# Scores as three fp32r products, exponentials kept in PSUM, and the last weights stored by chunk, in the cross attention of a fused perceiver block

## The chip, the cores and the metric

The kernel runs on one core of a Trainium2 chip. The metric is device time in microseconds (us), lowest is best, as the median of several runs. TensorE (PE in the profile) multiplies, VectorE (DVE), ScalarE (ACT) and GpSimd (POOL) work element by element, and SyncE (SP) issues nearly all DMAs.

## The reference

The whole function is a block on x of 64 batches x 32 rows x 512: a cross attention against a context of 257 rows x 128 per batch, then a self attention with small rank, then a feed-forward part. The change touches the cross attention alone. Cut to what matters, for one batch and 16 heads:

```python
q_big = rope(einsum("shk,hkq->shq", hidden_q @ Wq.T, w_kc_q))
kv_r  = rope(kv_c)                                  # 257 x 128
scores = einsum("hsr,hlr->hsl", q_big @ W_qr, kv_r @ W_kr)
attn  = softmax(scores, axis=-1)                    # over 257 positions
ctx_c = einsum("hsl,ld->hsd", attn, kv_r)           # 32 x 128 for each head
out   = concat_heads(ctx_c @ w_kc_kv.T) @ Wo.T      # 32 x 512, added to x
```

## The kernel before, in words

`query_path` (0 to 459 us) folds the query weights and both key weights, so that for every batch b there are finished queries of 128 x 512: 128 features on the partitions, 16 heads x 32 rows along the free side. They are written to an internal DRAM tensor (`carried_queries`), but the last two heads stay in SBUF, in `staged`, a part of `x1`. In its last units ACT copies the last two heads of batches 0 and 1 straight into `crossing.q` (L565). `fp32r` is a 4-byte format that TensorE multiplies in one pass; an fp32 product is kept accurate with it by splitting each operand into a rounded high part and a rest (low), and adding three products, high x high, high x low and low x high: `multiply_parts` (L65).

`cross_attention` (460 to 964 us) goes through 64 batches in 16 tiles of four (u = 0 to 3). A batch has two halves (steps); n = 2b + half counts the 128 steps. A step handles 8 heads as two blocks c of 128 rows. TensorE's program for step n is, in this order:

- `score(n+1)` (L1061): two fp32 matmuls, 128 queries x 257 keys, into two PSUM banks of `sc_ps`. Four banks exist, so steps alternate between two pairs. It waits for the exponentials of step n-1.
- `turn_weights(n)` (L1071): four transposes of the normalised weights `e` (positions 0 to 255) into `et_ps`. It waits for `normed` of n and for `et_split` of n-1.
- in half 1 `turn_kv` of the next batch; then a share of the output projection of an earlier tile (3 heads in half 1, 1 head in half 0, nine or three fp32r matmuls of 512 columns), and in half 0 `mix` of the batch before (six fp32r matmuls).

VectorE's program for step n: `find_peak(n+1)` (L892), `keep_ends(n)` (L906, the weight of position 256 out of `e`), in half 0 `split_kv`, in half 1 `add_end` of the batch before (L922, which adds position 256's share and needs its weights spread over all partitions), `normalise(n+1)` (L897), `split_turned(n)` (L913), and once in a tile `add_out` (L932). ScalarE's: `exponential(n+1)` (L997), `round_turned(n)` (L1006), in half 1 `round_kv` and `round_mixed` (L1018). GpSimd turns the keys of batch b + 2 in half 0 (`rotate`, L861, three operations) and makes the low part of the mixed values in half 1 (`split_mixed`, L872). SyncE (L829) issues in order for each batch: the store of the end weights of four batches back (2 KB, L821), three loads of raw keys (L707), the spread of those end weights out of DRAM to 128 partitions (L827), two loads of queries (L840, L841); once in a tile a load of x. After the last tile it issues five loads of weights for the self attention into `spare` (`holo.load`, L674), and only then the stores and spreads of the last four batches. All engines run their queues strictly in order, and nothing is planned by cost: the order is written out by hand.

Raw keys have four buffers, queries four, turned keys four, `ends` and `ends_spread` two.

Of the kernel before, what the change touches and what calls it, by code (L numbers as in the profile page):

```python
# [18 lines left out]
ALU = mybir.AluOpType  # L19
ACT = mybir.ActivationFunctionType  # L20
# [59 lines left out]
def query_path(nc, x_s, early, w_qr, w_kr, late, angle_q, centre_q, x1, spare, crossing, ident, eps, w_vo_dram, q_dram):  # L80
# [7 lines left out]
    with ExitStack() as ctx:  # L88
# [80 lines left out]
        def _(sp):  # L169
# [91 lines left out]
            crossing.output_weights(sp, w_vo_dram, 2)  # L261

# [252 lines left out]
        def _(act):  # L515
# [43 lines left out]
            def store_qc(U, J, sign):  # L559
                base = BASES[J][sign]  # L560
                for ab in range(2):
                    act.wait_ge(carried, 4 * U + 2 * sign + ab + 1)
                    if isinstance(U, int) and U >= 2 * HPAIRS - 2:
                        at = (H - 2 + ab) * S + base
                        nc.scalar.activation(crossing.q[:, :, at:at + G], ps[:, QC_BANK + ab].rearrange("p (b s) -> p b s", b=B)[:, 0:2], ACT.Copy)  # L565
# [117 lines left out]
class Crossing:  # L683


    def __init__(self, nc, ctx, cache_t, rope_kv):
# [4 lines left out]
        raw, swapped = sb("c_raw", [P, 2, L]), sb("c_swapped", [P, 2, L])  # L691
        self.raw, self.swapped = ([a[:, u] for u in range(2)] for a in (raw, swapped))

        self.q = sb("c_q_first", [P, 2, H * S])
        self.keys = sb("c_keys_first", [P, L])
        self.q_loaded = [sem(f"c_q_loaded{u}") for u in range(BT)]
        self.pool_chained, self.rotated = sem("c_pool_chained"), sem("c_rotated")
        self.table_loaded = sem("c_table_loaded")
        self.raw_loaded = [sem(f"c_raw_loaded{u}") for u in range(BT)]
# [14 lines left out]
    def first_queries(self, sp, q_dram):  # L714

        for u in range(2):
            sp.dma_start(self.q[:, u, 0:(H - 2) * S], q_dram[u, :, 0:H - 2].rearrange("d h s -> d (h s)")).then_inc(self.q_loaded[u], 16)
# [8 lines left out]
    def rotate_first(self, nc, pool, part):  # L726
# [3 lines left out]
        nc.gpsimd.tensor_tensor(part[:, 1], self.swapped[0], self.table[:, 1], ALU.mult).then_inc(self.pool_chained, 1)  # L730
        pool.wait_ge(self.pool_chained, 2)
        nc.gpsimd.tensor_tensor(self.keys[:], part[:, 0], part[:, 1], ALU.add).then_inc(self.rotated, 1)
# [7 lines left out]
def cross_attention(nc, crossing, holo, x, q_dram, w_vo_dram, ends_dram, x1, stat, ident, eps, half_pi, left_counted):  # L740
# [4 lines left out]
    with ExitStack() as ctx:  # L745
# [7 lines left out]
        raw_later, swapped_later = sb("c_raw_later", [P, BT - 2, L]), sb("c_swapped_later", [P, BT - 2, L])  # L753
        crossing.raw += [raw_later[:, u] for u in range(BT - 2)]
        crossing.swapped += [swapped_later[:, u] for u in range(BT - 2)]
        table, raw, swapped = crossing.table, crossing.raw, crossing.swapped
        table_loaded, raw_loaded = crossing.table_loaded, crossing.raw_loaded
        part = sb("c_part", [P, 2, L])
        kv_later = sb("c_kv_t", [P, BT - 1, L])
# [38 lines left out]
        def queries_in(u, t):  # L798

            return 32 * t + (16 if u < 2 else 32)  # L800
# [1361 lines left out]
```

## Time and profile before

| | us |
|---|---|
| median of 3 runs | 1603.71 (1599.01 to 1604.7) |
| the profiled execution: own time / span | 1602.14 / 1600.3 |
| mean granted TensorE clock of it | 0.972 |
| PE / DVE / ACT / POOL busy | 1482.6 / 1151.1 / 810.9 / 514.5 |
| cross attention, first scores to last projection | 460 to 964 |

The profile is of one execution. A share of busy time is an average over very different stages, and matmuls are pipelined, so their recorded durations overlap: the pace is read from the distance between two starts. A row of the timeline has the start, the time covered, the engine, the line of the code, what is written and read, and how many instructions were merged into it. An fp32 matmul shows as two records.

### The profile page before, as it was taken

Reading aid. Unit: us, or ns where it says so; the run is one execution under the profiler, and the core shown is the slowest. Engines: PE = TensorE matmul, PEld = TensorE weight load, DVE = VectorE, ACT = ScalarE, POOL = GpSimd, SP = SyncE. Lnnn points to the kernel's source line nnn. Section 1 sums busy time; section 2 is a strip of 40 time slices with the busy share of each in tenths; the row PEclk is TensorE's granted clock in tenths of the full one; section 3 lists DMA queues with packets and bytes.
Section 4 is the critical chain, followed back from the end, with each engine's and each line's share of the span. In section 5 each row is a group of like instructions: output and inputs, shape, how many; then the busy total and the mean of one; then the engine's idle time right before and its main releaser. Section 6 shows DMA issues by size and latency. Waiting matters only on the chain. (4 is left out here: it accounts for less than half of the span.)

```text
span 1600.3 us, 26575 instructions
## 1 busy us (share of the span) xinstructions
PE 1482.6 (93%) x8136; PEld 1122.0 (70%) x8136; DVE 1151.1 (72%) x2076; ACT 810.9 (51%) x1739; POOL 514.5 (32%) x466
## 2 busy tenths in 40 slices
PE   5799999999967999999999977999898899999997
PEld 3577777777746778777787756888443478787876
DVE  6888777887649888888888753767687735656466
ACT  4566566656545555555555433555211355554554
POOL 4244333542024444444444313221351202222021
PEclk9899999999999999999999988999898899999999
DMA  4223334243575555555555514000244100000000
GB/s 153 70 83 107 105 110 125 73 123 90 187 210 117 114 120 111 131 108 125 112 121 115 127 20 172 0 0 0 84 175 159 43 1 1 27 1 26 0 27 27
DMA packets 140918, 140.06 MB, mean 88 GB/s; under 512 B 84150, under 2 KB 111926, under 8 KB 139708
## 3 DMA queue, kind: packets, MB, share of 16 engines
q1 hardware_dynamic: 140284, 138.54, 32.5%
q10 hardware_dynamic: 576, 0.81, 0.2%
q8 instruction: 29, 0.48, 0.1%
q14 instruction: 29, 0.24, 0.0%
HBM read 109.88 MB, written 27.39 MB: 86 GB/s over the span
## 5 line engine op out<-in xcount | busy, mean ns | idle before, releaser
L1002 ACT ACTIVATE c_e<-c_sc_ps,c_peak 128x257 f32<-128x257 f32 x256 | 119.6, 472 | 215.3 <-DVE c_peak L895 215.3
L874 POOL TENSOR_TENSOR c_mixed_low<-c_whole,c_mixed_high 128x512 fp32r<-128x512 f32 x64 | 81.6, 1275 | 256.8 <-ACT c_mixed_high L1022 256.8
L77 DVE TENSOR_TENSOR b_rot_parts_low<-b_rot,b_rot_parts_high 128x1536 fp32r<-128x1536 f32 x64 | 136.5, 2132 | 21.9 <-ACT b_rot_parts_high L541 21.9
L1578 PE MATMUL f_ps<-f_right,f_left 128*128 128x512 f32 x256 | 115.5, 613 | 8.7 <-ACT f_raw L1621 6.3
L278 POOL TENSOR_TENSOR b_turned_raw<-b_turn_part 128x384 f32<-128x384 f32 x32 | 70.0, 2189 | 164.4 <-DVE b_key_parts_low L77 163.2
L895 DVE TENSOR_REDUCE c_peak<-c_sc_ps 128x2 f32<-128x514 f32 x128 | 88.5, 691 | 44.9 <-PE c_sc_ps L1068 43.4
L70 PE MATMUL c_out_ps<-c_shared_high,c_mixed_high 128*128 128x512 f32 x256 | 112.4, 439 | 8.5 <-issue 8.5
L324 DVE TENSOR_TENSOR b_rot<-b_w_qr,b_angle 128x1536 f32<-128x1536 f32 x64 | 118.6, 1852 | 0.2
L70 PE MATMUL b_ps<-c_shared_high,b_wq_parts_high 128*128 128x512 f32 x256 | 108.4, 423 | 6.5 <-DVE c_shared_low L77 6.5
L70 PE MATMUL e_mm_ps<-folded_high,e_h_t_high 128*128 128x512 f32 x256 | 106.4, 416 | 5.7 <-DVE e_h_t_low L77 5.6
L541 ACT ACTIVATE b_rot_parts_high<-b_rot 128x1536 fp32r<-128x1536 f32 x64 | 95.2, 1488 | 24.5 <-PE b_ps L72 17.0
L274 POOL TENSOR_TENSOR b_turn_part<-b_early,b_centre 128x384 f32<-128x384 f32 x64 | 83.8, 1329 | 71.5 <-DMA b_early<-early 69.9
L1934 ACT ACTIVATE spare<-spare 128x512 f32<-128x512 f32 x64 | 46.3, 724 | 114.0 <-DVE spare L2001 114.0
L72 PE MATMUL b_ps<-c_shared_high,b_wq_parts_low 128*128 128x512 f32 x256 | 103.5, 404 | 0.0
L1076 PE MATMUL c_et_ps<-ident,c_e 128*128 128x128 f32 x512 | 79.6, 278 | 25.8 <-DVE c_e_t_low L77 24.8
L71 PE MATMUL b_ps<-c_shared_low,b_wq_parts_high 128*128 128x512 f32 x256 | 103.0, 402 | 0.0
L72 PE MATMUL e_mm_ps<-folded_high,e_h_t_low 128*128 128x512 f32 x256 | 102.6, 401 | 0.0
L71 PE MATMUL e_mm_ps<-folded_low,e_h_t_high 128*128 128x512 f32 x256 | 102.4, 400 | 0.0
L71 PE MATMUL c_out_ps<-c_shared_low,c_mixed_high 128*128 128x512 f32 x256 | 102.3, 400 | 0.0
L72 PE MATMUL c_out_ps<-c_shared_high,c_mixed_low 128*128 128x512 f32 x256 | 102.3, 400 | 0.0
L1578 PEld LDWEIGHTS f_ps<-f_right,f_left 128*128 128x128 f32 x256 | 50.1, 197 | 73.9 <-issue 65.2
L1076 PEld LDWEIGHTS c_et_ps<-ident,c_e 128*128 128x128 f32 x512 | 57.1, 141 | 60.5 <-DVE c_e L903 31.3
(232 smaller groups left out, 3937.2 us busy)
## 6 DMA issues: line engine op xcount, KB each, us to landing
c_ends_spread<-end_weights SPq DMA_DIRECT2D x64, 256.0 KB, 3.8
carried_queries<-x SPq DMA_DIRECT2D x7, 2048.0 KB, 11.3
b_early<-early SPq DMA_DIRECT2D x15, 640.0 KB, 4.0
f_left<-ent_in SPq DMA_DIRECT2D x16, 512.0 KB, 5.2
f_right<-ent_out SPq DMA_DIRECT2D x16, 512.0 KB, 6.5
c_q_first<-carried_queries SPq DMA_DIRECT2D x32, 224.0 KB, 3.3
c_q<-carried_queries SPq DMA_DIRECT2D x32, 224.0 KB, 3.4
b_late<-late SPq DMA_DIRECT2D x16, 320.0 KB, 3.8
```

What stands on the lines that cost most here:

```text
L70: nc.tensor.matmul(out, left[0], right[0], start=start, stop=False)
L71: nc.tensor.matmul(out, left[0], right[1], start=False, stop=False)
L72: return nc.tensor.matmul(out, left[1], right[0], start=False, stop=stop)
L77: return nc.vector.tensor_tensor(low, value, high.bitcast(F32), ALU.subtract)
L274: nc.gpsimd.tensor_tensor(turn_part[:, n], key, centre[:, 2 * v + n].unsqueeze(2).to_broadcast(shape), ALU.mult).then_inc(key_multiplied, 1)
L324: nc.vector.tensor_tensor(rot[:, k % 2], weight, angles, ALU.mult).then_inc(rot_ready, 1)
L541: nc.scalar.activation(rot_parts[0][:, k % 2], rot[:, k % 2], ACT.Copy).then_inc(rot_rounded, 1)
L874: nc.gpsimd.tensor_tensor(mixed[1][:, w, :, u], whole[:, u % 2].rearrange("p (h s) -> p h s", h=H), mixed[0][:, w, :, u].bitcast(F32), ALU ...
L895: nc.vector.tensor_reduce(peak[:, v], sc_ps[:, 2 * v:2 * v + 2, 0:L], AX_X, ALU.max, negate=True).then_inc(peaked, 1)
L1002: last = nc.scalar.activation(e[:, v, c], sc_ps[:, 2 * v + c, 0:L], ACT.Exp, bias=peak[:, v, c:c + 1], accum_out=total[:, v, c:c + 1])
L1076: last = nc.tensor.transpose(et_ps[:, (2 * k + c) * P:(2 * k + c + 1) * P], e[:, half, c, k * P:(k + 1) * P], ident[:])
L1578: return nc.tensor.matmul(ps[:, m], left[:, slot, m * P:(m + 1) * P], right[:, slot], start=k == 0, stop=k == CF - 1)
```

## The change

It makes the score product out of fp32r parts: ScalarE rounds queries and keys (`round_queries`, `round_keys`), GpSimd makes the low parts (`split_queries`, in place of the loaded queries, and `split_keys`), and `score` is three products of 258 columns (257 and a zero) for each block. The exponentials overwrite the scores in PSUM; `normalise` becomes one operation from PSUM, and the end weights are taken from PSUM. The banks are now free for `score` only after `normed` and `ended` of the step two back. Raw keys have two buffers in place of four, and `part` moves into `spare`, so `holo.load` waits for the last rotation. The end weights are stored chunk by chunk (4-byte pieces), and `add_end` reads the spread ones without a stride. The last two heads of batches 0 and 1 come by DMA from `staged` after the last copy of the stage before. The sine argument steps at the end use three scratch pieces in place of two.

```diff
@@ query_path: sync, end
             crossing.output_weights(sp, w_vo_dram, 2)
+            sp.wait_ge(qc_stored, 8 * HPAIRS)
+            crossing.staged_queries(sp, staged)
@@ query_path: scalar
-                    if isinstance(U, int) and U >= 2 * HPAIRS - 2:
-                        at = (H - 2 + ab) * S + base
-                        nc.scalar.activation(crossing.q[:, :, at:at + G], ...)
@@ Crossing
-        self.raw_loaded = [sem(f"c_raw_loaded{u}") for u in range(BT)]
+        self.raw_loaded = [sem(f"c_raw_loaded{u}") for u in range(2)]
+    def staged_queries(self, sp, staged):
+        for u in range(2):
+            sp.dma_start(self.q[:, u, (H - 2) * S:].bitcast(F32), staged[:, u].rearrange("p h s -> p (h s)")).then_inc(self.q_loaded[u], 16)
@@ cross_attention: sync
-                sp.dma_start(ends_dram[bass.ds(b, 1)].rearrange("b p c -> p (b c)"), ends[:, v]).then_inc(ends_stored[v], 16)
+                sp.dma_start(ends_dram[bass.ds(b, 1)].rearrange("b c p -> p (b c)"), ends[:, v], allow_slow_non_contiguous=True).then_inc(ends_stored[v], 16)
                     if known(i, 1):
                         store_ends(i - 1, u)
-                        wait(sp, rotated_, b - BT + 1)
-                        crossing.load(sp, b, u)
+                    wait(sp, rotated_, b - 1)
+                    crossing.load(sp, b, u % 2)
+                    if known(i, 1):
                         spread_ends(i - 1, u)
...
             in_tiles(sp, tile)
+            sp.wait_ge(rotated_, B)
             holo.load(sp, holo_loaded)
@@ gpsimd
+            def split_queries(b, u):
+                pool.wait_ge(q_rounded, b + 1)
+                nc.gpsimd.tensor_tensor(q[u], q[u].bitcast(F32), q_high[:, u % 2].bitcast(F32), ALU.subtract).then_inc(q_split, 1)
+            def split_keys(b, u):
+                pool.wait_ge(key_rounded, b + 1)
+                nc.gpsimd.tensor_tensor(keys[1][:, u % 2], kv_even[u], keys[0][:, u % 2].bitcast(F32), ALU.subtract).then_inc(key_split, 1)
+            nc.gpsimd.memset(kv_later[:, :, L:], 0.0).then_inc(crossing.padded, 1)
+            split_keys(0, 0)
+            split_queries(0, 0)
             rotate(1, 1, 0)
+            split_keys(1, 1)
+            split_queries(1, 1)
             def tile(i, w):
+                    if half == 0 and not (isinstance(b, int) and (b == 0 or b + 1 >= B)):
+                        split_keys(b + 1, (u + 1) % BT)
                     if half == 0 and not (isinstance(b, int) and b + 2 >= B):
                         rotate(b + 2, (u + 2) % BT, i + (u + 2) // BT)
+                    if half == 1 and not (isinstance(b, int) and b + 2 >= B):
+                        split_queries(b + 2, (u + 2) % BT)
@@ vector: normalise, keep_ends, add_end
-                for c in range(2):
-                    last = nc.vector.tensor_scalar(e[:, v, c], e[:, v, c], inverse[:, v, c:c + 1], None, ALU.mult)
+                wait(dve, turned, n - 1)
+                nc.vector.tensor_tensor(e[:, v], sc_ps[:, 2 * v:2 * v + 2, 0:END], inverse[:, v].unsqueeze(2).to_broadcast([P, 2, END]), ALU.mult).then_inc(normed, 1)
-                dve.wait_ge(normed, n + 1)
-                nc.vector.tensor_copy(ends[:, v, 2 * half:2 * half + 2], e[:, half, :, END]).then_inc(ended, 1)
+                nc.vector.tensor_tensor(ends[:, v, 2 * half:2 * half + 2], sc_ps[:, 2 * half:2 * half + 2, END], inverse[:, half], ALU.mult).then_inc(ended, 1)
-                spread = ends_spread[:, v].rearrange("p (x c) -> p c x", c=CH)
+                (by_chunk(ends_spread[:, v]) takes its place)
@@ scalar
-                wait(act, turned, n - 1)
-                wait(act, ended, n - 1)
-                    last = nc.scalar.activation(e[:, v, c], sc_ps[:, 2 * v + c, 0:L], ACT.Exp, ...)
+                    last = nc.scalar.activation(sc_ps[:, 2 * v + c, 0:L], sc_ps[:, 2 * v + c, 0:L], ACT.Exp, ...)
+            def round_queries(b, u, t):
+                act.wait_ge(q_loaded[u], queries_in(u, t))
+                wait(act, scored, 2 * b - 2)
+                nc.scalar.activation(q_high[:, u % 2], q[u].bitcast(F32), ACT.Copy).then_inc(q_rounded, 1)
+            def round_keys(b, u):
+                act.wait_ge(rotated_, b + 1)
+                wait(act, scored, 2 * b - 2)
+                nc.scalar.activation(keys[0][:, u % 2], kv_even[u], ACT.Copy).then_inc(key_rounded, 1)
@@ scalar: at the end of each step, for batch b + 2
+                        if half == 0: round_queries(...)
+                        else: round_keys(...)
@@ scalar, before the tiles
+            round_keys(0, 0)
+            round_queries(0, 0, 0)
             exponential(0, 0)
             round_kv(0, 0)
+            round_keys(1, 1)
+            round_queries(1, 1, 0)
@@ tensor: score
-                    pe.wait_ge(q_loaded[u], queries_in(u, t))
-                    pe.wait_ge(rotated_, b + 1)
-                wait(pe, exped, n - 1)
+                    pe.wait_ge(q_split, b + 1)
+                    pe.wait_ge(key_split, b + 1)
+                wait(pe, normed, n - 1)
+                wait(pe, ended, n - 1)
-                    last = nc.tensor.matmul(sc_ps[:, 2 * half + c, 0:L], q[u][:, at], kv_t[u], start=True, stop=True)
+                    last = multiply_parts(nc, sc_ps[:, 2 * half + c, 0:LE], [q_high[:, u % 2, at], q[u][:, at]], [a[:, u % 2] for a in keys], True, True)
```

## Rows read from the trace of the kernel before

**Rows 1.** Timeline of TensorE, one tile: scores (L1068), transposes (L1076); start, us.
```profile
671.26 1.03 PE L1068 MATMUL c_sc_ps<-c_kv_t,c_q_first 128*128 128x257 f32 x4
...
675.06 1.03 PE L1068 MATMUL c_sc_ps<-c_kv_t,c_q_first 128*128 128x257 f32 x4
675.92 0.60 PE L1076 MATMUL c_et_ps<-ident,c_e 128*128 128x128 f32 x4
...
678.45 1.03 PE L1068 MATMUL c_sc_ps<-c_kv_t,c_q 128*128 128x257 f32 x4
679.47 0.63 PE L1076 MATMUL c_et_ps<-ident,c_e 128*128 128x128 f32 x4
...
682.24 1.03 PE L1068 MATMUL c_sc_ps<-c_kv_t,c_q 128*128 128x257 f32 x4
683.48 0.63 PE L1076 MATMUL c_et_ps<-ident,c_e 128*128 128x128 f32 x4 [0.21 <-DVE c_e_t_low L77]
...
700.35 1.03 PE L1068 MATMUL c_sc_ps<-c_kv_t,c_q_first 128*128 128x257 f32 x4
```
**Rows 2.** Timeline of TensorE, two fp32r matmuls of 512 columns, 18 apart.
```profile
959.72 0.40 PE L72 MATMUL c_out_ps<-c_shared_high,c_mixed_low 128*128 128x512 f32 x1
...
963.92 0.40 PE L72 MATMUL c_out_ps<-c_shared_high,c_mixed_low 128*128 128x512 f32 x1
```
**Rows 3.** Timeline of TensorE, fp32 matmuls of 128 columns, and what follows them.
```profile
994.63 2.05 PE L1242 MATMUL d_ps<-d_xn_t,d_basis 128*128 128x128 f32 x16
996.51 1.02 PE L1293 MATMUL d_ps<-spare 128*128 128x512 f32 x2
```
**Rows 4.** Timeline of VectorE, in the same tile.
```profile
676.12 0.69 DVE L895 TENSOR_REDUCE c_peak<-c_sc_ps 128x2 f32<-128x514 f32 x1 [0.59 <-PE c_sc_ps L1068]
...
678.11 0.62 DVE L903 TENSOR_SCALAR c_e<-c_e,c_inverse 128x257 f32<-128x257 f32 x2
```
**Rows 5.** Groups by line and form, 560 to 960 us: busy, mean ns | idle before.
```profile
L903 DVE TENSOR_SCALAR c_e<-c_e,c_inverse 128x257 f32<-128x257 f32 x202 | 68.2, 380 | 3.5
...
L874 POOL TENSOR_TENSOR c_mixed_low<-c_whole,c_mixed_high 128x512 fp32r<-128x512 f32 x53 | 67.6, 1276 | 208.4 <-ACT c_mixed_high L1022 208.4
...
L1022 ACT ACTIVATE c_mixed_high<-c_whole 128x512 fp32r<-128x512 f32 x52 | 33.6, 646 | 10.5 <-DVE c_whole L929 10.5
```
**Rows 6.** Timeline, store of end weights, their spread, and their use in `add_end`.
```profile
702.36 0.36 SPq L821 DMA_DIRECT2D end_weights<-c_ends  x1
...
704.84 0.45 SPq L827 DMA_DIRECT2D c_ends_spread<-end_weights  x1
...
709.90 1.12 DVE L929 SCALAR_TENSOR_TENSOR c_whole<-c_ends_spread,c_keys_first,c_mix_ps 128x512 f32<-128x512 f32 x1
```
**Rows 7.** DMA queue, 703.1 to 703.6 us: packets, MB, share of 16 engines.
```profile
q1 hardware_dynamic: 144, 0.00, 15.5%
```
**Rows 8.** DMA issues of the page: count, KB each, median us to landing.
```profile
c_ends_spread<-end_weights SPq DMA_DIRECT2D x64, 256.0 KB, 3.8
...
carried_queries<-x SPq DMA_DIRECT2D x7, 2048.0 KB, 11.3
...
end_weights<-c_ends SPq DMA_DIRECT2D x64, 2.0 KB, 1.4
...
c_shared_low<-output_weights_low SPq DMA_DIRECT2D x1, 512.0 KB, 4.5
```
**Rows 9.** Timeline, start of the cross attention.
```profile
459.02 0.43 SPq L724 DMA_DIRECT2D c_shared_low<-output_weights_low  x1
...
460.05 2.05 PE L1068 MATMUL c_sc_ps<-c_keys_first,c_q_first 128*128 128x257 f32 x4 [2.53 <-PEq L88]
```
**Rows 10.** Timeline, its end: first late load, last rotation, the late `add_end`.
```profile
907.72 1.71 SPq L676 DMA_DIRECT2D spare<-phase_nat  x1
...
912.31 0.64 POOL L869 TENSOR_TENSOR c_kv_t<-c_part 128x257 f32<-128x257 f32 x1
...
919.28 1.11 DVE L929 SCALAR_TENSOR_TENSOR c_whole<-c_ends_spread,c_keys_first,c_mix_ps 128x512 f32<-128x512 f32 x1 [3.84 <-issue]
```

More of the change, by code:

```diff
@@ L752, in cross_attention @@
         END = L - 1
[L753 to L755 removed]
         table, raw, swapped = crossing.table, crossing.raw, crossing.swapped
         table_loaded, raw_loaded = crossing.table_loaded, crossing.raw_loaded
[L758 to L760 removed]
+        part = spare[:, 0:2 * L].rearrange("p (n l) -> p n l", n=2)
+        LE = L + 1
+        kv_later = sb("c_kv_t", [P, BT - 1, LE])
+        kv_even = [crossing.keys[:]] + [kv_later[:, u] for u in range(BT - 1)]
+        kv_t = [a[:, 0:L] for a in kv_even]
         kv = pair("c_kv", [P, BT, 2, P])
[L762 removed]
+        q_later = sb("c_q", [P, BT - 2, H * S], F32R)
         q = [crossing.q[:, u] for u in range(2)] + [q_later[:, u] for u in range(BT - 2)]
+        q_high = sb("c_q_high", [P, 2, H * S], F32R)
+        keys = pair("c_key", [P, 2, LE])
         peak = sb("c_peak", [P, 2, 2])
@@ L782, in cross_attention @@
         q_loaded, rotated_, pool_chained = crossing.q_loaded, crossing.rotated, crossing.pool_chained
+        q_rounded, q_split, key_rounded, key_split = (sem(f"c_{n}") for n in ("q_rounded", "q_split", "key_rounded", "key_split"))
         kv_turned, kv_rounded, kv_split = (sem(f"c_{n}") for n in ("kv_turned", "kv_rounded", "kv_split"))
@@ L798, in queries_in @@
         def queries_in(u, t):
-            return 32 * t + (16 if u < 2 else 32)
+            return 32 * (t + 1)
         def in_tiles(engine, tile):
@@ L846, in tile @@
                              x_tiles[bass.ds(i, 1)].rearrange("t p d -> p (t d)")).then_inc(x_loaded, 16)
-            for u in range(2, BT):
-                crossing.load(sp, u, u)
             in_tiles(sp, tile)
+            sp.wait_ge(rotated_, B)
             holo.load(sp, holo_loaded)
@@ L909, in keep_ends @@
                     wait(dve, ends_stored[v], 32 * i + 16 * (u // 2))
-                dve.wait_ge(normed, n + 1)
-                nc.vector.tensor_copy(ends[:, v, 2 * half:2 * half + 2], e[:, half, :, END]).then_inc(ended, 1)
+                nc.vector.tensor_tensor(ends[:, v, 2 * half:2 * half + 2], sc_ps[:, 2 * half:2 * half + 2, END], inverse[:, half],
+                                        ALU.mult).then_inc(ended, 1)
             def split_turned(n, u, half):
@@ L1041, in tile @@
                         round_mixed(b - 1, (u - 1) % BT, i if u else i - 1, w if u else 1 - w)
+                    if not (isinstance(b, int) and b + 2 >= B):
+                        if half == 0:
+                            round_queries(b + 2, (u + 2) % BT, i + (u + 2) // BT)
+                        else:
+                            round_keys(b + 2, (u + 2) % BT)
                     if j == 4 and known(i, 2):
```

62 lines of the change are left out of this document (33 added, 29 removed).

## The prediction

> **What bounds the kernel now.** I read the table of busy times first: PE is busy 1482.6 us of 1600.3, DVE 1151.1, but these are averages, and the change touches one stage, the cross attention from 460 to 964 us. So next the timeline of one tile of it. In [rows 1] TensorE needs 0.86 us for one step's scores (675.06 to 675.92), then runs the transposes, and from their start to the next scores pass 2.53 us (675.92 to 678.45, one projection head and a mix) or 2.77 us (679.47 to 682.24, three heads and the key transposes). 2.53 + 2.77 + 2 x 0.86 = 7.02 us is TensorE's own work for a batch. The tile takes 700.35 - 671.26 = 29.09 us, 7.27 for a batch. The rest, 0.25, is waiting ahead of the transposes: those at 679.47 could have started at 678.45 + 0.86 = 679.31, those at 683.48 at 683.10. They wait for the low part of the weights turned a step earlier, the end of a chain through all engines: scores, peak, exponentials, reciprocal, normalisation, low part. From the end of a step's scores (675.92) to the next step's transposes (679.47) it lasts 3.55 us. So two limits lie close together, TensorE's queue and this chain, and I need both for the sum. The rule: transposes start at the later of the end of the scores ahead of them, and the end of the scores before those plus 3.55.
>
> For a pair of steps this gives 3.55 + 2.77 + 0.86 = 7.18: the chain binds in the first step, the queue in the second. **A faster score product therefore counts once in a batch, and a longer chain counts once too.**
>
> **Score product.** Two fp32 matmuls of 257 columns take 0.86 us. Six fp32r matmuls of 258 take their place. No row has fp32r at that width. [Rows 2]: 18 matmuls of 512 columns in 4.20 us, 233 ns each, and by columns 258/512 of that is 118 ns. From the other side, [rows 3]: 16 records in 1.88 us (994.63 to 996.51), 118 ns each; each record passes 256 columns (an fp32 matmul shows as two, and 257 columns took 0.86/4 = 215 ns a record, so about two passes of 257), with a weight load ahead of each, as here. If the 20 ns by which 233 exceeds 215 are a fixed cost, it is 127. I take 120: 0.72 us a step, 0.14 less. Ends: 0.70, and 6 x 0.233 = 1.40 should width not count at all.
>
> A rule speaks against this part: the Trainium skill, "TensorE: Matmul & The Clock Gate", part 3 (The mechanism), says that a weight load overlaps running matmuls only when it goes to other row groups. Here all loads fill the whole array, and six loads replace four. Its figure for a load of 128 columns, 107 ns, would give an estimate of 6 x (107 + 108) = 1.29 us. The trace disagrees: [rows 3] have such a pair each 118 ns.
>
> **Normalisation.** Two SBUF operations (0.62 us for both, [rows 4]) become one of 512 elements out of PSUM. The nearest row is the peak, 514 elements from PSUM, 0.69 [rows 4]. So the chain grows by 0.07, to 3.62. Ends: 0 and 0.14. The old form has some stretched cases: in [rows 5] 202 of them are busy 68.2 us, 0.675 a pair, 0.055 over 0.62. These are the ones beside a GpSimd operation. The peak shows no such stretch, and I let it vanish.
>
> The Trainium skill explains this in "VectorE: DVE Perf Modes" (The perf-mode tier table): single-source fp32 from SBUF runs at twice the rate, anything from PSUM does not. By that the new form would take as long as the peak; the row agrees.
>
> **Exponentials in PSUM.** No row has ScalarE writing PSUM. I take no change; ends -0.05 and +0.05 for each of the two, so -0.10 to +0.10 on the chain. The Trainium skill ("ScalarE: Activation LUTs", Step-by-step) calls PSUM the faster destination; no row here shows it. The waits that go (turned, ended) were for events a whole step old, and those that come for the scores (normed and ended of two steps back) are also old: normalisation and end weights of step n-1 run in VectorE's step n-2 and n-1. Nothing for either.
>
> **`add_end` and end weights.** `add_end` takes 1.12 us [rows 6], because it reads every fourth word; contiguous it should take about the 0.69 of the peak. But in its step it runs while ScalarE makes the exponentials, and the reciprocal after it waits for these anyway. So 0.4 us of VectorE, 0 of time, once per batch. The two-element end weights lie in the same shadow.
>
> **New work on ScalarE and GpSimd.** Per batch ScalarE gets a rounding of 512 elements (0.65 [rows 5]) and one of 258 (about 0.4), behind everything else of a step, 1.05 in 7.27 with the engine near half busy. Behind them waits the next exponential, which today starts after idle time. GpSimd gets 1.28 [rows 5] and about 0.75: with the rotation (three of about 0.75) and `split_mixed` 5.6 us of 7.2. It fits, hidden; if a key split came too late TensorE would wait in the scores of half 0.
>
> **The tile by the rule** (scores 0.72, chain 3.62): transposes at 0, then 3.62 (chain), 7.71 (in this step `add_out` delays the peak: old 7.56 in [rows 1], plus 0.15 for two longer normalisations), 11.00, 14.62, 18.13, 21.63, 25.25 and 28.75. Old: 29.09. **0.34 us for a tile, 5.1 for 15.** The old tile held one stretched normalisation, 0.31 us; the mean is 8 x 0.055 = 0.44, which adds 0.13 x 15 = 2.0. Loop: **-7**. With the ends above (scores 0.70 to 0.76, chain 3.45 to 3.75): -18 to +2.
>
> **Store in 4-byte pieces.** 512 packets in place of 128. In [rows 7] 144 small packets take 15.5% of 16 x 0.5 us = 1.24 us, 8.6 ns each; 32 for each engine instead of 8 add 0.2 us. Upper end: the 256-byte pieces of `carried_queries` [rows 8], 8192 in 11.3 us over 16 engines, 22 ns each: +0.5. The store lands after 1.4 [rows 8], the spread is issued 2.48 us after it [rows 6], because SyncE issues three loads between them; so 0.9 of cover. The spread lands 3.8 later [rows 8], its user starts 709.90 - 704.84 = 5.06 after; other batches have less. Cost 0. SyncE also waits, between store and loads, for the rotation of two batches on; behind that wait stand the loads and the spread. GpSimd ends this rotation in half 0 and the store comes a step later, so it is past by about 1 us even with a key split ahead. Cost 0; a late rotation would cost as a late store does.
>
> **Start.** The last two query heads of batch 0 now come by DMA, issued after the 512 KB weight load of 459.02, in whose queue they stand. That load lands at 459.02 + 4.5 = 463.5 [rows 8, 9], the queries about 463.9. Then rounding 0.65, the low part 1.28, releases 0.2: scores at 466.0 in place of 460.05 [rows 9]. **+6.0**. Ends: +3.5, if the small transfer passes the large, and +8.
>
> **End.** The late weight loads start at 907.72 now, and everything behind them in SyncE's queue (the store and spread of batch 60) makes `add_end` wait until 919.28 [rows 10], 3.84 of it idle. New, the loads wait for the last rotation: its last operation ends at 912.95, plus one key split ahead of it 0.75, so 913.8, 6.1 later. The first issue took 1.71 where the DMA queue was full, so some is won back: **+5.5** (4.5 to 7), less 0.4 for the faster `add_end`, which lies open here. The three scratch pieces of the sine steps have the same elements: 0.
>
> **Sum**, against the profiled execution's own time: 1602.1 + 6.0 + 5.5 - 0.4 - 7 = 1606.2. It stands 1.6 below the median of the runs shown, 1603.71, well inside their spread; the change is +4.1. Between the two bases I forecast 1607.
>
> **Rivals.** (A) *The fixed costs don't show in full and the chain is shorter.* ScalarE is quicker into PSUM by 0.05 each, so chain -0.10: 6 us more in the loop; start +3.5: 1607 - 6 - 2.5 = 1598; with more stretched steps gone, 1592. For it: the waiting ahead of transposes is chain, not queue. Against: the normalisation lengthens it. (B) *Slower: the spread comes too late.* The place is `add_end` in half 1, in front of `normalise`, so each us of delay goes straight into the chain. It decides once the store takes 0.9 + about 0.5 us more than now, that is over 50 ns for a 4-byte packet. At 100 ns: 32 x 0.1 - 0.8 = 2.4 later, 1 us behind, times 60 batches: 1667. At the edge, in a third of the batches by 0.5: +10, 1617. Against it are the 8.6 ns; for it, that four times as many pieces go to DRAM in one line. (C) *The matmuls of 258 columns are not cheap* (weight loads open, or width not counted): 1.29 to 1.40 in place of 0.72, 0.57 to 0.68 a step, less the slack of the chain; 2.53 + 2.77 + 2.6 = 7.9 a batch, +0.6 x 62: about 1650. (D) *The change doesn't do what it says:* GpSimd or ScalarE, in order, hold back `key_split` or an exponential by 0.3 in each batch: 1625.
>
> **Chances.** Forecast 0.48, A 0.20, B 0.16 (mostly its edge), C 0.06, D 0.10. What a measurement of this kernel can tell from no change is 0.5%, 8 us: 1595.7 to 1611.7. The forecast's own range is 1597 to 1616. Faster 0.19, same 0.46, slower 0.35. The range 1592 to 1626 leaves out C, the strong form of B and little of A.
>
> **What would show it.** Start to start, the fp32r score matmuls at 118 to 127 ns; scores to transposes 0.72 us plus waiting; transposes in half 1 still held by the low part; normalisation 0.69 with no stretched case; `add_end` about 0.69 without idle time before it; the first scores near 466; the first late load 6 us later, measured from the last rotation; batches of 7.19 in place of 7.27. A DMA named as the releaser of `add_end`, a key or query split of GpSimd ahead of the scores, or a start below +3 would make it wrong.

## The result and the profile after

The changed kernel takes 1943.43 us (median of 4 runs, 1936.95 to 1946.81); the kernel before, on the same chip, 1602.1. The ratio is 1.2129, 95% interval 1.2106 to 1.2152. The forecast of 1607 is wrong by 336 us, and the time lies far outside the range. All of the difference is in the cross attention: the last `add_end` comes at 1287.6 us instead of 941.9, and what follows keeps its length.

The page of the changed kernel, busy times and the slices of PE and of its clock:

```profile
span 1943.8 us, 27410 instructions
...
PE 1569.2 (81%) x8392; PEld 1215.6 (63%) x8392; DVE 1110.5 (57%) x1952; ACT 870.8 (45%) x1859; POOL 633.9 (33%) x596
...
PE   5899999996466766676667766558998898999998
...
PEclk8999999997787777878888788888999898999999
```

From slice 10 on PE is six tenths busy and its clock falls. What it waits for is in the waits of the stretch from 600 to 900 us (what waited and for what: us in total, times, longest):

```profile
DVE c_whole L956 <- DMA c_ends_spread<-end_weights: 64.1, 15, 5.6
...
DVE c_whole L956 <- issue: 36.7, 9, 5.0
...
SPq L837 <- DMA end_weights<-c_ends: 174.2, 23, 9.8
SPq L831 <- DVE c_ends L938: 0.4, 1, 0.4
```

So VectorE stands ahead of `add_end` in each of the 24 batches of this stretch (12.5 us a batch instead of 7.3), and the spread it waits for is itself held in SyncE's queue until the store has landed. The nine waits put down to "issue" are of the same kind: they too end 3.5 to 5.4 us after the issue of the spread, like the other fifteen (3.8 to 5.4). The DMA issues of the same stretch (count, KB, median us to landing) and SyncE's timeline of one batch:

```profile
end_weights<-c_ends SPq DMA_DIRECT2D x24, 2.0 KB, 9.9
...
c_raw<-cache_t SPq DMA_DIRECT2D x24, 128.5 KB, 6.8
```

```profile
793.76 0.42 SPq L831 DMA_DIRECT2D end_weights<-c_ends  x1
794.37 0.35 SPq L710 DMA_DIRECT2D c_raw<-cache_t  x1
794.90 1.13 SPq L713 DMA_DIRECT2D c_swapped<-cache_t  x2
803.86 0.34 SPq L837 DMA_DIRECT2D c_ends_spread<-end_weights  x1
804.49 0.34 SPq L851 DMA_DIRECT2D c_q_first<-carried_queries  x1
804.98 0.53 SPq L852 DMA_DIRECT2D c_q_first<-x  x1
805.78 0.41 SPq L831 DMA_DIRECT2D end_weights<-c_ends  x1
```

The store of 2 KB lands after 9.9 us where it took 1.4 [rows 8], the spread is issued 10.1 us behind it where it was 2.48 [rows 6] (means of 600 to 900 us: 10.1 and 2.6), and then come `add_end` and, behind it, the chain of the other engines. VectorE and TensorE, just after:

```profile
808.91 0.75 DVE L956 SCALAR_TENSOR_TENSOR c_whole<-c_ends_spread,c_kv_t,c_mix_ps 128x512 f32<-128x512 f32 x1 [3.71 <-issue]
...
809.77 0.69 DVE L931 TENSOR_TENSOR c_e<-c_sc_ps,c_inverse 128x512 f32<-128x512 f32 x1
810.38 0.68 DVE L77 TENSOR_TENSOR c_e_t_low<-c_et_ps,c_e_t_high 128x512 fp32r<-128x512 f32 x1
```

```profile
807.00 0.28 PE L70 MATMUL c_sc_ps<-c_key_high,c_q_high 128*128 128x258 f32 x1
807.12 0.28 PE L71 MATMUL c_sc_ps<-c_key_low,c_q_high 128*128 128x258 f32 x1
...
811.21 1.09 PE L1124 MATMUL c_et_ps<-ident,c_e 128*128 128x128 f32 x4 [3.33 <-DVE c_e_t_low L77]
811.95 0.78 PE L70 MATMUL c_out_ps<-c_shared_high,c_mixed_high 128*128 128x512 f32 x1
```

Here one also reads that the score matmuls are 120 ns apart, the normalisation takes 0.69 and `add_end` 0.75: the parts that I priced from rows came out. One that I priced at nothing did not.

### The profile page after: what moved, and what is told of

Its sections match the earlier page's. It is cut to its first block and busy times, and to the rows that moved or that the text cites. A ratio compares the mean times of both kernels' runs of the same rounds, so it can differ in the third digit from the quotient of the medians.

```text
span 1943.8 us, 27410 instructions
## 1 busy us (share of the span) xinstructions
PE 1569.2 (81%) x8392; PEld 1215.6 (63%) x8392; DVE 1110.5 (57%) x1952; ACT 870.8 (45%) x1859; POOL 633.9 (33%) x596
## 5 line engine op out<-in xcount | busy, mean ns | idle before, releaser
L1124 PE MATMUL c_et_ps<-ident,c_e 128*128 128x128 f32 x512 | 100.7, 331 | 265.8 <-DVE c_e_t_low L77 264.8
L1124 PEld LDWEIGHTS c_et_ps<-ident,c_e 128*128 128x128 f32 x512 | 70.6, 169 | 278.1 <-DVE c_e L931 277.9
L1030 ACT ACTIVATE c_sc_ps<-c_sc_ps,c_peak 128x257 f32<-128x257 f32 x256 | 113.6, 444 | 245.4 <-DVE c_peak L923 245.2
L956 DVE SCALAR_TENSOR_TENSOR c_whole<-c_ends_spread,c_kv_t,c_mix_ps 128x512 f32<-128x512 f32 x48 | 35.9, 747 | 202.0 <-issue 119.7
L1060 ACT ACTIVATE c_mixed_high<-c_whole 128x512 fp32r<-128x512 f32 x64 | 40.3, 630 | 231.4 <-DVE c_whole L956 231.4
L70 PE MATMUL c_out_ps<-c_shared_high,c_mixed_high 128*128 128x512 f32 x256 | 125.6, 491 | 10.8 <-issue 10.8
L72 PE MATMUL c_out_ps<-c_shared_high,c_mixed_low 128*128 128x512 f32 x256 | 113.3, 443 | 0.0
L71 PE MATMUL c_out_ps<-c_shared_low,c_mixed_high 128*128 128x512 f32 x256 | 113.2, 442 | 0.0
```

Source lines behind the costliest of these rows:

```text
L70: nc.tensor.matmul(out, left[0], right[0], start=start, stop=False)
L71: nc.tensor.matmul(out, left[0], right[1], start=False, stop=False)
L72: return nc.tensor.matmul(out, left[1], right[0], start=False, stop=stop)
L1030: last = nc.scalar.activation(sc_ps[:, 2 * v + c, 0:L], sc_ps[:, 2 * v + c, 0:L], ACT.Exp, bias=peak[:, v, c:c + 1], accum_out=total[:, v, ...
L1124: last = nc.tensor.transpose(et_ps[:, (2 * k + c) * P:(2 * k + c + 1) * P], e[:, half, c, k * P:(k + 1) * P], ident[:])
```

## Experiments

**Is it the store?** The changed kernel with only its store and spread as before, and the kernel before with only the 4-byte store.

```diff
 # e1_wide_store, against the changed kernel
-sp.dma_start(ends_dram[...].rearrange("b c p -> p (b c)"), ends[:, v], allow_slow_non_contiguous=True)
+sp.dma_start(ends_dram[...].rearrange("b p c -> p (b c)"), ends[:, v])
-    by_chunk(whole[:, v]), by_chunk(ends_spread[:, v]), ...
+    by_chunk(whole[:, v]), ends_spread[:, v].rearrange("p (x c) -> p c x", c=CH), ...
 # (the spread's view of end_weights and its shape in DRAM are turned with it)
 # e2_before_narrow: the same lines the other way round, in the kernel before
```

> The changed kernel with one part undone: end weights are stored in 16-byte pieces again (128 of them), spread in that order, and read with a stride by add_end. Theory (the store in 4-byte pieces): the loss is all in the wait of add_end for the store; the store lands after about 1.4 us again, batches take 7.2 to 7.3 us instead of 12, and the sum of the prediction holds: 1600 to 1615 us. Rival (two raw-key buffers and the new order of waits on SyncE hold the spread back as well): store-to-spread stays above 4 us and the time above 1650. Rival (the in-order work put on GpSimd and ScalarE): batches of 7.6 to 8 us, 1625 to 1650.

> The kernel before with one part of the change alone: end weights stored chunk by chunk in 4-byte pieces (512 of them), spread in that order, read without a stride. Theory (the store): 1900 to 1960 us, store-to-spread about 10 us, add_end idle ahead. Rival (the store is slow only together with the new order of loads): below 1700.

Measured: with the wide store 1605.68 us, ratio 1.0023 (1.0012 to 1.0034); the kernel before with the narrow store 1931.46, ratio 1.2048 (1.2012 to 1.2083). The store alone makes nearly all of the loss, in either kernel, and the rest of the change comes to +3.7 us by the ratio (1.9 to 5.4), where the prediction had +4.1.

**What is slow about it?** Stores and loads by themselves, issued by SyncE one after the other. The first kernel:

```diff
+("rows16",  (P, CH),      lambda a: a)                              # 128 rows of 16 bytes
+("dense4",  (CH, P),      lambda a: a.rearrange("c p -> p c"))      # 512 pieces of 4, side by side
+("apart64", (CH, P, 16),  lambda a: a[:, :, 0].rearrange("c p -> p c"))
+go(again["dense4"][r]...); go(loads[1][:], x[0:P, 0:257])           # a load behind the store
```

> No part of the reference's computation: x is copied to the output, and between lie small DMAs from SyncE, each awaited alone. Forms of a store to DRAM: 128 pieces of 16 bytes; 512 of 4 bytes side by side; 256 of 8; 128 of 4; 512 of 4 bytes put 64 bytes or 512 bytes apart; 128 of 4, 64 bytes apart. Then a load of 128 x 1028 bytes alone, behind the 16-byte store and behind the 4-byte store. Theory A (pieces that fall into the same small stretch of DRAM are written one after the other): side by side about 8 to 10 us, 64 or 512 bytes apart 2 to 3 us, 128 of 4 bytes side by side about 3 to 4. Theory B (each small piece costs by itself, wherever it goes): all three forms of 512 alike, 8 to 10 us, 256 pieces half of that. Theory C (issuing or making the pieces is slow): the packets themselves come late. The load behind the 4-byte store lands late under A and B (over 6 us), at 3 us under C only if packets come late.

The rows of its issues (the dots stand for other forms; a name's digits are dropped, so `apart` is a pitch of 64 and of 512 bytes together):

```profile
alone_load<-x SPq DMA_DIRECT2D x4, 128.5 KB, 2.0
behind_rows_load<-x SPq DMA_DIRECT2D x4, 128.5 KB, 4.1
behind_dense_load<-x SPq DMA_DIRECT2D x4, 128.5 KB, 11.7
...
apart<-tile SPq DMA_DIRECT2D x12, 2.0 KB, 1.9
rows<-tile SPq DMA_DIRECT2D x6, 2.0 KB, 1.4
...
dense_again<-tile SPq DMA_DIRECT2D x4, 2.0 KB, 9.2
```

The same 512 pieces of 4 bytes land after 1.9 us when they lie 64 bytes or more apart, and after 9.2 side by side. So it is neither the number of packets nor their size. That was theory A of the expectation; theory B, by which all forms of 512 pieces cost alike, is out. A load issued behind the slow store lands after 11.7, behind the 16-byte one after 4.1.

> Stores by themselves, one after the other, each form six times; the kernel copies its input to its output and leaves the whole computation out. All write 4-byte pieces unless said otherwise: side by side in DRAM (neighbours come from different partitions), with a pitch of 8, 16 and 32 bytes, side by side with four neighbours from one partition, 256 pieces of 8 bytes, 128 pieces of 4 bytes side by side, and rows of 16 bytes. Theory: pieces that share a small block of DRAM and come from different partitions wait for each other, so the time falls with the pitch: 9.4 us side by side, about 3 at pitch 8 (as 8-byte pieces), 2.5 at pitch 16, 2 at pitch 32; with four neighbours from one partition it stays well below 9.4, near 3. Rival (each 4-byte piece inside a used block costs, whoever writes it): four neighbours from one partition take 9 us as well, and a pitch of 16 or 32 bytes changes little until the pieces lie in blocks of their own.

```profile
side_by_side<-tile SPq DMA_DIRECT2D x6, 2.0 KB, 9.1
pitch_eight<-tile SPq DMA_DIRECT2D x6, 2.0 KB, 3.9
pitch_sixteen<-tile SPq DMA_DIRECT2D x6, 2.0 KB, 3.0
pitch_thirtytwo<-tile SPq DMA_DIRECT2D x6, 2.0 KB, 2.0
own_neighbours<-tile SPq DMA_DIRECT2D x6, 2.0 KB, 7.1
pieces_of_eight<-tile SPq DMA_DIRECT2D x6, 2.0 KB, 3.0
one_in_line<-tile SPq DMA_DIRECT2D x6, 0.5 KB, 7.4
whole_rows<-tile SPq DMA_DIRECT2D x6, 2.0 KB, 1.4
```

The time falls with the pitch, as the theory says and the rival doesn't. But four neighbours from one partition take 7.1, where the theory had about 3 and the rival 9: that different partitions write them is the smaller part. Neither of the two is borne out whole. And 128 pieces in one line take 7.4 (theory A had 3 to 4) where 512 in four lines take 9.1, so it doesn't go by number either: what lies close together counts. Where does the time go? The DMA queue in two stretches of this kernel's first store, which is issued at 14.62 and followed by the next at 23.55: first 14.6 to 16.6, then 16.6 to 19 (the stretch 19 to 23.5 answers in the same way).

```profile
q1 hardware_dynamic: 528, 0.00, 12.6%
...
DMA packets 0, 0.00 MB, mean 0 GB/s; under 512 B 0, under 2 KB 0, under 8 KB 0
```

12.6% of 16 x 2.0 us are 4.0 us for 528 packets, 7.6 ns each: shorter than the 8.6 that I took from [rows 7]. They are through in 2 us, and then for 7 us the queue has nothing to do and the store has not landed. Whatever it still waits for, a packet's time does not hold it. That the writes have to be confirmed is a likely reason; no run shows it.

The Trainium skill says of this, "DMA: Bandwidth & Descriptors", in its Anatomy of one DMA, that the semaphore is raised only when the last byte is confirmed in the target memory, surprisingly late at times when that is HBM. That section describes DMAs issued by GpSimd, and these are SyncE's. In its Specifications it says that below 512 bytes a read-modify-write takes place. By the section's fixed cost of about 2.0 us both stores would be alike; the runs have 1.4 and 9.1, so the sentence on the confirmation is compatible with them and the figure does not hold for neighbours. The read-modify-write is a likely reason for what the pitch does; no run shows it.

**How much later may the store land?** A dose between the two: pieces of 8 bytes.

```diff
 # e9_pieces_of_eight, against e1_wide_store
+ends_dram = nc.dram_tensor("end_weights", (B, H // HG // 2, P, 2), F32, kind="Internal").ap()
+sp.dma_start(ends_dram[...].rearrange("b c p k -> p (b c) k"), ends[:, v].rearrange("p (c k) -> p c k", k=2), ...)
 # (the spread follows, and add_end becomes two instructions of 256 elements)
```

> The wide-store kernel with the end weights of a batch stored as 256 pieces of 8 bytes (two rows of 1 KB) instead of 128 of 16, and add_end in two halves for it. The same store measured by itself takes 3.1 us from issue to issue against 1.6 for the 16-byte form and 9.4 for 4-byte pieces. Theory: only the landing time of the store counts, and 1.5 us more lie in the shadow (0.9 us until SyncE's three loads are issued, and part of a microsecond ahead of add_end); the rest is small: 1606 to 1625. Rival: what costs is the scattered store as such, by its number of packets (half of the 4-byte form's): then half of the 338 us or more shows, above 1750.

Measured: 1634.39 us, ratio 1.0196 (1.018 to 1.0212), 9 us above the theory's range and far from the rival's. The store lands after 3.9 us, not 3.1, and the waits of 600 to 900 us show that 37 of 40 `add_end` now stand:

```profile
DVE c_whole L958 <- DMA c_ends_spread<-end_weights: 24.5, 25, 1.9
...
DVE c_whole L958 <- issue: 6.8, 12, 0.9
...
SPq L831 <- DVE c_ends L938: 55.4, 39, 2.3
```

2.5 us more of landing cost (1.0196 - 1.0023) x 1602 / 60 = 0.46 us a batch, and 8.5 us more cost 5.6. So the first 2 us or so are covered. Between the two doses 6.0 us more of landing cost 5.2 more: behind the cover most of each microsecond counts. `add_end` in two instructions is a second difference of this kernel (0.48 us each, 0.96 in place of 1.13), and no run takes it apart from the store.

**Which loop binds: SyncE's queue, or the way of the data?**

```diff
 # e10_spread_last, against the changed kernel, SyncE's tile
-                    if known(i, 1):
-                        spread_ends(i - 1, u)
                     wait(sp, scored, 2 * (b - BT) + 2)
                     ... # the two query loads
+                    if known(i, 1):
+                        spread_ends(i - 1, u)
```

> The changed kernel, 4-byte store kept; SyncE issues the two query loads of a batch ahead of the wait for the store and the spread, instead of behind them. Theory (SyncE's queue is the loop): a batch lasts as long as SyncE needs from one store to the next, 10.1 us until the store has landed and 1.9 for the spread, the two query loads and the way to the next store; with the query loads ahead the 1.9 become about 0.6, so a batch takes 10.7 us instead of 12.0 and the kernel 1943 - 1.3 x 60 = about 1865. Rival (the data's way is the loop: end weights, store, spread, add_end, next end weights): the order in SyncE's queue is indifferent and the time stays within 10 us of 1943.

Measured: 1972.99 us, ratio 1.2313 (1.2293 to 1.2332). My theory falls: SyncE's step from spread to store did shrink, to 0.6 us where nothing else held the store, and the kernel became slower. The rival's range, within 10 us of 1943, is missed too. Its timeline, SyncE and VectorE:

```profile
788.33 0.41 SPq L831 DMA_DIRECT2D end_weights<-c_ends  x1
...
798.63 0.34 SPq L837 DMA_DIRECT2D c_ends_spread<-end_weights  x1
799.23 0.41 SPq L831 DMA_DIRECT2D end_weights<-c_ends  x1
...
812.20 0.41 SPq L831 DMA_DIRECT2D end_weights<-c_ends  x1
```

```profile
803.73 0.75 DVE L956 SCALAR_TENSOR_TENSOR c_whole<-c_ends_spread,c_keys_first,c_mix_ps 128x512 f32<-128x512 f32 x1 [8.00 <-DMA c_ends_spread<-end_weights]
...
811.88 0.15 DVE L938 TENSOR_TENSOR c_ends<-c_sc_ps,c_inverse 128x2 f32<-128x2 f32 x1
```

The store of 788.33 leads to `add_end` at 803.73; two steps of VectorE later the end weights of two batches on are made, 811.88, and their store goes at 812.20. That is 23.87 us for two batches, 11.9 for one, and it has nothing of SyncE's order in it. SyncE's own loop in the changed kernel was 12.0 in the batch shown above (793.76 to 805.78), without waiting for end weights (0.4 us in 300 there, 23.7 here). These are single batches; from 600 to 900 us the means are 12.5 us a batch in the changed kernel and 12.7 here. In the changed kernel SyncE's queue is the loop that binds; the data's way lies close beside it, both hang on the landing, and shortening one moves the wait to the other. What SyncE gains between spread and store (1.5 us on average instead of 2.5) it loses between store and spread, 11.1 instead of 10.1: the store's landing is waited for longer, probably because the two query loads are now issued behind it, and they themselves land after 10.6 us (4.5 in the changed kernel, `c_q`, 600 to 900 us). This balances to within 0.2 us a batch. It does not account for all of the 30 us, and that part stays open.

**The rest of the sum: end, start, scores.** All against the wide-store kernel or built on it.

```diff
 # e3_late_loads (and e6_before_late in the kernel before, which has no wait for rotated_), SyncE's tail
-            sp.wait_ge(rotated_, B)
-            holo.load(sp, holo_loaded)
             for u in range(BT):
+                if u == 2:
+                    sp.wait_ge(rotated_, B)
+                    holo.load(sp, holo_loaded)
                 store_ends(TILES - 1, u)
 # e4_queries_first = e3 and:
+            crossing.staged_queries(sp, staged)
             crossing.output_weights(sp, w_vo_dram, 2)
-            crossing.staged_queries(sp, staged)
 # e8_queries_direct = e4 and, for batch 0, ScalarE copies the heads as in the kernel before,
 # into an fp32 tile c_q_plain; the low part goes to c_q_low_first
 # e5_fp32_scores = e1, without rounding and splitting of keys and queries, and:
-    multiply_parts(nc, sc_ps[:, 2 * half + c, 0:LE], [q_high..., q...], [a[:, u % 2] for a in keys], True, True)
+    nc.tensor.matmul(sc_ps[:, 2 * half + c, 0:L], q[u][:, at], kv_t[u], start=True, stop=True)
```

> The changed kernel with the wide store (16-byte rows), and in the last four batches SyncE issues the stores and spreads of the first two before it waits for the last rotation and issues the late weight loads. Theory: with the wide store all that is left of the change's cost is at the start (+8 us: first scores 467.6 instead of 460.1) and at the end (5.5 us, the spread stands behind the wait for the rotation, add_end of batch 60 comes 18 us after the one before it); here the end's cost goes, and with it the 3.8 us that the kernel before loses there as well: 9 us below the wide-store kernel (1605.7), about 1596.5. Rival: the late loads themselves, or the stage after the cross attention, set the end; then the time stays within 2 us of 1605.7. Second rival: the loads come too late for the next stage, and the time is above 1606.

> The kernel before, changed in one place: in the last four batches SyncE issues the stores and spreads of the first two before the late weight loads. Theory: the 3.84 us that add_end of batch 60 stands idle, and what the batch behind it loses, go: 4 to 6 us below the kernel before, about 1597. Rival: the end is set by the next stage's loads, which now come later: within 1 us of the kernel before, or slower.

> The kernel with wide store and late loads, and the two query heads of batch 0 that now come by DMA are issued ahead of the last 512 KB weight load instead of behind it. Theory: the start costs because the small transfer stands behind the large one in SyncE's queue; ahead of it the heads land about 2.5 us sooner and the first scores come at about 465 instead of 467.6: 2.5 us less than the kernel with late loads, about 1594. Rival: the start is set by the rounding, the split and the keys' way through ScalarE and GpSimd; then nothing is gained (within 0.5 us).

> The kernel with wide store, late loads and the staged queries ahead of the weight load, and ScalarE once more copies the last two query heads of batch 0 straight from PSUM (into an fp32 tile of their own, with the low part in another one); only batch 1's come by DMA. It splits the start. Theory: of the 6 us that the first scores come late after the last key product, about 3.5 are the way of the two heads by SyncE and DMA (landed near 465.4) and the rest rounding and splitting (466.06 to 468.17 in the trace of the kernel before this one); so the first scores come some 5.8 us after the last key product instead of 9.3, and the time is 3 us less, about 1591.5. Rival: the table load of ScalarE and the low part of the keys hold the scores as long as the DMA does; then below 1 us is gained, about 1594.

> The wide-store kernel with the scores as two fp32 products of 257 columns again, and without rounding and splitting keys and queries; exponentials in PSUM, the single normalisation and the contiguous end weights stay. It isolates the score products. Theory (the sum of the prediction): a step's scores take 0.86 us instead of 0.72, which counts once a batch: 0.14 x 62 = 9 us more in the loop, less some 4 us at the start, where rounding and splitting go; so 1605.7 + 5 = about 1610. Rival 1: the chain of peak, exponentials and normalisation binds in both steps and the score products are free: loop unchanged, only the start is won back, about 1601. Rival 2: the splits on GpSimd and the rounding on ScalarE cost something in each batch: below 1600.

The ratios are each to the kernel before, run beside it (1601.7, 1601.6 or 1603.4 us).

| kernel | us | ratio to before, 95% | expected |
|---|---|---|---|
| wide store | 1605.68 | 1.0023 (1.0012 to 1.0034) | 1600 to 1615 |
| + late loads | 1596.57 | 0.9964 (0.995 to 0.9978) | 1596.5 |
| before + late loads | 1596.55 | 0.9968 (0.9955 to 0.9981) | 1597 |
| + late loads, queries first | 1594.73 | 0.9954 (0.9937 to 0.9971) | 1594 |
| + and batch 0 direct | 1592.53 | 0.9933 (0.9919 to 0.9946) | 1591.5 |
| wide store, fp32 scores | 1609.21 | 1.0048 (1.0032 to 1.0064) | 1610 |

The end: `add_end` of batch 60 in the wide-store kernel and with late loads:

```profile
925.16 1.12 DVE L956 SCALAR_TENSOR_TENSOR c_whole<-c_ends_spread,c_keys_first,c_mix_ps 128x512 f32<-128x512 f32 x1 [10.22 <-issue]
```

```profile
913.63 1.11 DVE L957 SCALAR_TENSOR_TENSOR c_whole<-c_ends_spread,c_keys_first,c_mix_ps 128x512 f32<-128x512 f32 x1
```

The idle 10.22 us are gone, and 9.4 us of them in the time (0.9964 against 1.0023). In the kernel before, whose idle time there is 3.84 [rows 10], the same edit gives 5.1. The difference, 4.3 (plus or minus about 3.5 by the intervals), is the change's own price at the end. The queries ahead of the weight load give 1.6 us, but the two intervals overlap: not told apart from nothing. The direct copy gives 3.4 more by the ratios, where 3 were expected, but here too the intervals overlap; only the two steps together, 5.0 us, are clear of noise. And the trace does not bear out how I had split the start:

```profile
456.83 1.13 PE L464 MATMUL b_ps<-spare,b_w_kr 64*128 64x512 f32 x4 [1.40 <-ACT x L568]
...
461.32 1.28 ACT L1096 ACT_TABLE_LOAD   x1 [2.14 <-PEq L88]
...
462.72 0.40 ACT L1062 ACTIVATE c_key_high<-c_keys_first 128x258 fp32r<-128x258 f32 x1
463.03 0.61 ACT L1057 ACTIVATE c_q_high<-c_q_plain 128x512 fp32r<-128x512 f32 x1
...
463.89 1.27 POOL L897 TENSOR_TENSOR c_q_low_first<-c_q_plain,c_q_high 128x512 fp32r<-128x512 f32 x1
...
465.21 0.58 PE L70 MATMUL c_sc_ps<-c_key_high,c_q_high 128*128 128x258 f32 x1 [7.25 <-POOL c_q_low_first L897]
```

From the last key product to the first scores pass 8.4 us (9.3 with the heads by DMA, 9.7 in the wide-store kernel, 3.66 before), not the 5.8 that I expected. The stage begins for all engines when SyncE has issued its last load, ScalarE then loads a table for 1.28 us, and only then come the roundings. In the kernel before this load lay beside the first scores; now it is ahead of them. As long as the heads come late by DMA (in the wide-store kernel the rounding of the keys ends at 464.8 and that of the queries waits until 465.6) most of it is hidden, and it shows once they don't.

With fp32 scores the kernel is 4.0 us slower than with fp32r scores, plus or minus about 3. From the first scores to `add_end` of batch 59 it needs 443.8 us (466.00 to 909.82), the wide-store kernel 439.5 (467.64 to 907.17), the kernel before 447.0 (460.05 to 907.07). Each of these is one execution, and executions of the wide-store kernel spread over 5 us, so differences of 3 or 4 us between them are rough. The expected 1610 was met by luck: 9 us more in the loop came to 4.3, and 4 us less at the start to 1.6.

## Why the prediction was wrong

**The step that failed is the store in 4-byte pieces, "cost 0".** It worked out the time that packets take, 8.6 ns each, and was right in that (7.6). It took for granted that the store lands when its packets are through. Measured alone, it lands 7 us after them. In the kernel it lands 8.5 us later than before; 2 to 3 of these are covered, and 5.6 a batch are left: 337 us by the ratios, the whole error.

**Rival B was the case that came.** Its place (`add_end`, ahead of `normalise`), its edge (more than 0.9 + 0.5 us of delay) and "each us of delay goes straight into the chain" are borne out in the main (0.86 of each us), and so is its reason, that the pieces go to DRAM in one line. The edge was somewhat low: 2.5 us of delay cost only 0.46 a batch. It had too small a size, 50 to 100 ns a packet, where the landing corresponds to 8.5 / 32 = 266, and it laid the cost to the packets, which take 7.6 ns as in the forecast. At 1667 it was still 276 us short. What misled me is that both bounds, 8.6 and 22 ns, are rates of packets. The rows that I had bound the throughput of a queue, and I had asked for a latency: no row of before showed a landing of small neighbouring pieces, so this cost had no upper end, and I gave it one.

There was also a view that told how much a late store may cost, and I did not read it: SyncE's waits in the kernel before, 600 to 900 us.

```profile
SPq L821 <- DVE c_ends L911: 106.8, 42, 3.8
SPq L827 <- DMA end_weights<-c_ends: 10.2, 11, 1.6
```

SyncE idles 106.8 / 42 = 2.5 us a batch ahead of the store: that is what its queue has to give. With it the size of the loss comes out, for SyncE's queue binds in the changed kernel: the spread goes out 10.1 - 2.6 = 7.5 us later behind the store, less 2.5 is 5.0 a batch, and the batches grew by 5.2 (7.3 to 12.5). The cover of a smaller delay is another one, that of the data's way. With pieces of 8 bytes SyncE still idles 55.4 / 39 = 1.4 us a batch ahead of the store, and `add_end` waits already. [Rows 6] and [rows 8] give that cover for one batch: 2.48 - 1.4 = 1.1 us until the spread is issued and 5.06 - 3.8 = 1.3 after it has landed, 2.3 in all.

**The other steps**, from the wide-store kernel:

- *Score product 0.72 a step*: 120 ns a matmul, as taken; six weight loads cost nothing that can be seen. So Rival C is out, and so is the rule as it was taken from the Trainium skill ("TensorE: Matmul & The Clock Gate", The mechanism): the same section also lets a load into the background weight buffer run ahead of matmuls, which the prediction left out and which agrees with the 120 ns. The fp32 version gives its worth: 4.3 us in the loop, where "once in a batch" would make 0.14 x 61 = 8.5. It counts about half, as far as single executions tell: TensorE's waits for the low part of the weights rise from 3.1 us (12 times, 600 to 900 us, before) to 9.5 (30 times) in the wide-store kernel, so the chain may take a part back.
- *Normalisation 0.69, exponentials 0, `add_end` hidden*: 691 ns; the exponential takes 444 ns into PSUM against 472 into SBUF before, 0.03 less each; the trace agrees here with the direction that the Trainium skill gives ("ScalarE: Activation LUTs", Step-by-step). These edits, together with the two raw-key buffers and the new order of waits, which no run takes apart, make the other 3.2 us (447.0 to 443.8), where the sum had a small loss apart from the stretched cases.
- *Loop -7*: -7.5, and batches of 7.18 us on average from 600 to 900 us, where 7.19 was forecast. The sum holds in part by luck, for its parts are shifted: the scores gave less and the rest more.
- *`add_end` 0.69 contiguous*: 0.75, in the changed kernel.
- *New work on ScalarE and GpSimd 0*: the wide-store kernel shows one wait of TensorE for GpSimd from 470 to 940 us, 1.0 us long. Rival D is out.
- *Start +6.0*: 9.72 against 3.66 from the last key product, +6.1. The size is right, the reason in part: the table load was missing, and its 1.28 us lie beside the DMA. In the span the first scores come at 467.64, 7.6 later than before, because the last key product is 1.5 later too.
- *End +5.5 - 0.4*: 4.3. The "full queue" behind the first issue's 1.71 us isn't borne out: the queue moved nothing in its first half microsecond. The five issues take 3.4 us in the wide-store kernel instead of 3.6, so next to nothing was won back.
- The sum of all but the store, forecast at +4.1, was measured at +3.7.

## What to carry to other kernels

Ask of a small transfer when it lands, not how long its packets take: if anything waits for it, measure its form by itself first. Never write 4-byte pieces side by side to DRAM on a path that something waits for; a row of 16 bytes for each partition lands after 1.4 us, and the stride moved to the reader costs VectorE 0.4 us (1.13 against 0.75); whether that is hidden no run shows by itself. Two covers bound what a later landing may cost, and both can be read beforehand: the idle time of the issuing queue ahead of its own waits, and the slack on the data's way, between landing and next issue and between landing and use. And loads for the next stage belong behind the stores that this stage still waits for: that gives 5 us in the kernel before and 9 in the wide-store kernel, and the best one here, with wide store, late loads and direct copy, is 0.67% faster than the kernel before.

## What the hardware did that I had not expected

- 2 KB to DRAM: 16-byte rows land after 1.4 us, 4-byte pieces with a pitch of 32 bytes 2.0, of 16 bytes 3.0, of 8 bytes 3.9, side by side 9.1. In each of these 4-byte forms the first store shows 528 packets, and they are through 2.2 us after the issue. 128 pieces side by side take 7.4.
- A load behind such a store in SyncE's queue lands after 11.7 us instead of 4.1 behind a wide one.
- TensorE's clock: the granted clock of 600 to 900 us is 1.00 before, the level of 2.4 GHz, and 0.81 after, a mean of both levels. In the rows above TensorE idles 3.33 us, and a 512-column matmul just behind it is recorded at 0.78 us where [rows 2] have 0.40; the granted clock from 811.9 to 812.8 us is 0.50, the level of 1.2 GHz. That this costs time isn't shown: SyncE's queue sets the pace there and waits 0.4 us in 300 for end weights, so the slower TensorE seems to fit into the wait.
